# Layer two's experts: the product between the two halves comes out turned, with the first weights copied into fixed buffers and the expert's number loaded once per tile on VectorE

## The chip, the cores and the metric

The kernel runs on one core of a Trainium2 chip. The metric is the device time of one execution in microseconds (us). Engines are named as in the profile: PE (TensorE matmul), PEld (its weight loads), DVE (VectorE), ACT (ScalarE), POOL (GpSimd), SP (SyncE).

## What is computed

Four layers, each an attention and a feed-forward part, run over 32 sequences of 128 tokens with 128 features, all in float32. The change touches the feed-forward part of layer two, a mixture of eight experts of which each token uses the likeliest:

```
logits = jnp.einsum('bsd,de->bse', x, router_W) + router_b
probs = jax.nn.softmax(logits, axis=-1)
gates = one_hot(argmax(probs), 8) * probs
h = jax.nn.relu(jnp.einsum('bsd,edf->besf', x, W1) + b1[:, None, :])   # W1: 8 x 128 x 512
y = jnp.einsum('besf,efd->besd', h, W2) + b2[:, None, :]               # W2: 8 x 512 x 128
out = jnp.einsum('bse,besd->bsd', gates, y)
```

## The kernel before

Layer two (`layer2`) first does its attention for eight groups of four sequences, routes each token, and scatters the normalised token rows, sorted by expert, into `sorted_x` in DRAM. Each expert's rows fill whole tiles of 128 rows, so there are NTILE = 32 + 8 - 1 = 39 tiles. DVE works out, for each tile, its expert's number (`te`, an int32 row in SBUF) and its first row (`row`).

Then the tile loop runs on all five engines at once, each with its own hand-written order and semaphores between them. For tile u:

- SP loads the tile's 128 rows (`xt`, four buffers) once `turn_x` of tile u-4 is done (L1481 to L1485).
- PE `turn_x` (L1639) transposes them; ACT `xT_out` (L1776) copies the result to SBUF (`xT`, three buffers).
- DVE `add_b1` (L2013) loads the expert's number (L2006), adds the bias row of the expert, held in SBUF as a copy on each of the 128 partitions, and writes `hp` (two buffers).
- PE `turn_h` (L1654) transposes `hp` in four blocks of 128 (one pass each) into `bankH`, and ACT (L1784) applies the relu on the way to `hT` in SBUF (two buffers).
- PE `down` (L1663) loads the expert's number and multiplies with `l2f_w2`: four products of 128 columns summed in PSUM, eight passes, with the weights' address worked out in a register before each product.
- DVE `add_b2` (L2021) loads the expert's number and adds the second bias; POOL (L1823) stores the tile (`yt`, two buffers) to `routed_y`.

PE's order in step u of its loop is up(u+2), turn_x(u+3), turn_h(u+1), down(u). DVE's is add_b1(u+2), add_b2(u), and behind add_b2(2) it does eight small operations for the routing (`gates_and_places`, L2025 to L2033). ACT's is the relu of u, then xT_out(u+3). Layer three starts behind a barrier of all engines at the end of layer two.

Of the kernel before, what the change touches and what calls it, by code (L numbers as in the profile page):

```python
# [70 lines left out]
def seq(c):  # L71
    return slice(c * P, (c + 1) * P)
# [1251 lines left out]
def layer2(nc, k):  # L1324

    with ExitStack() as ctx:
# [63 lines left out]
        NX, NXT = 4, 3  # L1390
        xt = sb("x_tile", [P, NX, P], F32)
        xT = sb("xT_tile", [P, NXT, P], F32)
        hp = sb("h_tile", [P, 2, HID], F32)
        hT = sb("hT_tile", [P, 2, HID], F32)
        yt = sb("y_tile", [P, 2, P], F32)
# [1 line left out]
        bankX, bankS, bankAT, bankA, bankO, bankX2, bankM, bankR = (k.bank(i) for i in range(8))  # L1397
        bankL, bankK = bankR[:, 0:GS * NE2], bankR[:, 256:256 + GS * NE2]
        bankXT, bankU = [k.bank(0), k.bank(7)], [k.bank(1), k.bank(2)]
        bankH, bankY = [k.bank(3), k.bank(4)], [k.bank(5), k.bank(6)]  # L1400

        s_fill = sem("fills_done")
        s_row = sem("bias_row_ready")
# [46 lines left out]
        s_xt = [sem(f"x_tile_in_{p}") for p in range(NX)]  # L1450
        s_turn = sem("x_tile_turned")
        s_xT = sem("xT_tile_ready")
        s_up = sem("h_in_psum")
        s_hp = sem("h_tile_ready")
        s_turnh = sem("h_tile_turned")
        s_hT = sem("hT_tile_ready")
        s_y = sem("y_in_psum")
        s_yt = sem("y_tile_ready")
# [29 lines left out]
        def _(pe):  # L1488
# [150 lines left out]
                pe.transpose(bankXT[u % 2][:, 0:P], xt[:, u % NX, :], k.ident[:, :]).then_inc(s_turn, 1)  # L1639

            def up(u):
                e = expert(u)
                pe.wait_ge(s_xT, u + 1)
                if u >= 2:
                    pe.wait_ge(s_hp, u - 1)
                pe.matmul(bankU[u % 2][:, :], xT[:, u % NXT, :], w["l2f_w1"][:, bass.ds(e * HID, HID)], start=True,  # L1646
                          stop=True).then_inc(s_up, 1)

            def turn_h(u):
                pe.wait_ge(s_hp, u + 1)  # L1650
                if u >= 2:
                    pe.wait_ge(s_hT, u - 1)
                for n in range(NHB):
                    ins = pe.transpose(bankH[u % 2][:, seq(n)], hp[:, u % 2, seq(n)], k.ident[:, :])  # L1654
                ins.then_inc(s_turnh, 1)

            def down(u):
                e = expert(u)
# [9 lines left out]
                turn_x(u)  # L1668
            up(0)
            up(1)  # L1670
            turn_h(0)
            for u in range(NTILE):
                if u + 2 < NTILE:
                    up(u + 2)
                if u + 3 < NTILE:
                    turn_x(u + 3)
                if u + 1 < NTILE:
                    turn_h(u + 1)
                down(u)

        @block.scalar
        def _(act):
            k.wait_weights(act, "l2x")

            def normalise(dst, g, shift, rstd):
                for c in range(GS):
                    ins = act.activation(dst[:, c, :], k.x_sb[:, seq(g * GS + c)], ACT.Identity,
                                         bias=shift[:, g % 2, c:c + 1], scale=rstd[:, g % 2, c:c + 1])
                return ins

            def xn_in(g):
                act.wait_ge(s_shift1, g + 1)
                if g >= 3:
                    act.wait_ge(s_hbp, g - 2)
                normalise(xn[:, g % 3, :, :], g, shift1, rstd1).then_inc(s_xn, 1)

            def xnT_out(g):
                act.wait_ge(s_xp, g + 1)
                if g >= 3:
                    act.wait_ge(s_o, g - 2)  # L1700
                act.activation(xnT[:, g % 3, :], bankX[:, :], ACT.Copy).then_inc(s_xnT, 1)
                if g >= 2:
                    act.wait_ge(s_s, g - 1)
                act.activation(hwT[:, g % 2, :], bankX[:, :], ACT.Identity, bias=w["l2x_w2"][:, :],
                               scale=w["l2x_w3"][:, :]).then_inc(s_hw, 1)

            def exps(g):
                act.wait_ge(s_nmax, g + 1)
                if g >= 1:
                    act.wait_ge(s_attn, g)  # L1710
                for c in range(GS):
                    ins = act.activation(probs[:, c, :], bankS[:, seq(c)], ACT.Exp, bias=nmax[:, g % 2, c:c + 1],
                                         accum_out=total[:, c:c + 1])
                ins.then_inc(s_p, 1)

            def token_exp(g):
                act.wait_ge(s_m4, g + 1)
                if g >= 1:
                    act.wait_ge(s_pwp, g)
                act.activation(e4[:, :], bankM[0:GS, 128:256], ACT.Exp, bias=m4[:, :], accum_out=z4[:, :])\  # L1720
                   .then_inc(s_e4, 1)

            def attnT_out(g):
                act.wait_ge(s_atp, g + 1)
                if g >= 1:
                    act.wait_ge(s_a, g)
                act.activation(attnT[:, :], bankAT[:, :], ACT.Copy).then_inc(s_at, 1)

            def aT_out(g):
                act.wait_ge(s_a, g + 1)  # L1730
                if g >= 1:
                    act.wait_ge(s_o, g)
                act.activation(aT[:, :], bankA[:, :], ACT.Copy).then_inc(s_aT, 1)

            def h2_in(g):
                act.wait_ge(s_shift2, g + 1)
                normalise(h_all[:, rows(g)].rearrange("p (c d) -> p c d", c=GS), g, shift2, rstd2).then_inc(s_h2, 1)

            def hT2_out(g):
                act.wait_ge(s_h2p, g + 1)  # L1740
                if g >= 1:
                    act.wait_ge(s_lg, g)
                act.activation(hT2[:, :], bankX2[:, :], ACT.Copy).then_inc(s_hT2, 1)

            def gate_exp(g):
                act.wait_ge(s_sh, g + 1)
                act.activation(ex[:, g % 2, :], sh[:, g % 2, :], ACT.Exp).then_inc(s_ex, 1)

            xn_in(0)
            xn_in(1)  # L1750
            xnT_out(0)
            for s in range(last_step):
                if s < NG:
                    exps(s)
                if 2 <= s < NG + 2:
                    hT2_out(s - 2)
                if s < NG:
                    token_exp(s)
                if s + 1 < NG:
                    xnT_out(s + 1)  # L1760
                if s < NG:
                    attnT_out(s)
                if s + 2 < NG:
                    xn_in(s + 2)
                if 2 <= s < NG + 2:
                    gate_exp(s - 2)
                if s < NG:
                    aT_out(s)
                if 1 <= s < NG + 1:
                    h2_in(s - 1)  # L1770

            def xT_out(u):
                act.wait_ge(s_turn, u + 1)
                if u >= NXT:
                    act.wait_ge(s_up, u - NXT + 1)
                act.activation(xT[:, u % NXT, :], bankXT[u % 2][:, 0:P], ACT.Copy).then_inc(s_xT, 1)  # L1776

            for u in range(3):
                xT_out(u)
            for u in range(NTILE):  # L1780
                act.wait_ge(s_turnh, u + 1)
                if u >= 2:
                    act.wait_ge(s_y, u - 1)
                act.activation(hT[:, u % 2, :], bankH[u % 2][:, :], ACT.Relu).then_inc(s_hT, 1)  # L1784
                if u + 3 < NTILE:
                    xT_out(u + 3)

# [40 lines left out]
        def _(dve):  # L1828
# [176 lines left out]
            def expert(u):  # L2005
                return dve.value_load(te[0:1, u:u + 1], min_val=0, max_val=NE2 - 1)  # L2006

            def add_b1(u):
                e = expert(u)
                dve.wait_ge(s_up, u + 1)  # L2010
                if u >= 2:
                    dve.wait_ge(s_turnh, u - 1)
                dve.tensor_tensor(hp[:, u % 2, :], bankU[u % 2][:, :], w["l2f_b1"][:, bass.ds(e * HID, HID)], ALU.add)\  # L2013
                   .then_inc(s_hp, 1)

            def add_b2(u):
                e = expert(u)
                dve.wait_ge(s_y, u + 1)
                if u >= 2:
                    dve.wait_ge(s_out[u % 2], 16 * (u // 2))  # L2020
# [3 lines left out]
            def gates_and_places():  # L2024
# [7 lines left out]
                step(dve.scalar_tensor_tensor(pos_f[:, :], skip_all[:, :], -float(P), pos_f[:, :], ALU.mult, ALU.add))  # L2032
                dve.tensor_copy(k.routed_pos[:, :], pos_f[:, :])  # L2033

            add_b1(0)
            add_b1(1)
            for u in range(NTILE):
                if u + 2 < NTILE:
                    add_b1(u + 2)
                add_b2(u)  # L2040
                if u == 2:
                    gates_and_places()
# [847 lines left out]
class Global(Core):  # L2890
# [78 lines left out]
    def wait_weights(self, eng, layer):  # L2969
# [8 lines left out]
    "l1x": {"l1x_" + n: s for n, s in ATTN.items()},  # L2978
    "l0f": {"l0f_w1": [P, HID], "l0f_w2": [P, NHB, P], "l0f_cw": [P, 3 * HID], "l0f_cb": [P, NHB]},
    "l2f": {"l2f_router": [P, NE2], "l2f_router_b": [P, GS * NE2], "l2f_w1": [P, NE2 * HID],  # L2980
            "l2f_b1": [P, NE2 * HID], "l2f_w2": [P, NE2 * HID], "l2f_b2": [P, NE2 * P]},
    "l2x": {"l2x_w1": [P, 1], "l2x_w2": [P, 1], "l2x_w3": [P, 1], "l2x_bsim": [P, 1], "l2x_wqv": [P, 4, P],
            "l2x_bqv": [P, P]},
    "l3r": {"l3f_sim": [P, NE3], "l3f_gates": [P, NE3]},
# [109 lines left out]
def layouts(i):  # L3094
# [26 lines left out]
    d["l2f_router"] = f(i["L2_ffn_router_W"])  # L3121
    d["l2f_router_b"] = f(np.tile(i["L2_ffn_router_b"].reshape(1, NE2), (1, GS)))
    d["l2f_w1"] = f(np.transpose(i["L2_ffn_W1"], (1, 0, 2)).reshape(P, NE2 * HID))
    d["l2f_b1"] = f(i["L2_ffn_b1"].reshape(1, NE2 * HID))
    d["l2f_w2"] = f(np.transpose(i["L2_ffn_W2"].reshape(NE2, NHB, P, P), (2, 0, 1, 3)).reshape(P, NE2 * HID))
    d["l2f_b2"] = f(i["L2_ffn_b2"].reshape(1, NE2 * P))

# [41 lines left out]
```

## Time and profile before

| | us |
|---|---|
| median of three runs (1568.3, 1568.77, 1574.62) | 1568.77 |
| the profiled execution, its whole time | 1566.59 |
| its span in the profile | 1564.6 |
| lies around the span | 1.99 |
| PE busy in the span | 1371.5 (88%) |
| DVE / ACT / POOL busy | 852.7 / 546.8 / 417.6 |
| mean granted clock of PE | 0.916 |
| the tile loop, first `up` (862.9) to last `down` (962.3) | 99.4 |

The profile has for each engine the busy time, and for each group of instructions the line, the mean duration and the idle time before it with what ended it. Records of matmuls overlap, since PE is a pipeline: of a row that merges n equal passes, the distance between two starts is (the row's length minus the length of one record) / (n - 1).
### The profile page before, as it was taken

Reading aid. Unit: us, or ns where it says so; the run is one execution under the profiler, and the core shown is the slowest. Engines: PE = TensorE matmul, PEld = TensorE weight load, DVE = VectorE, ACT = ScalarE, POOL = GpSimd, SP = SyncE. Lnnn points to the kernel's source line nnn. Section 1 sums busy time; section 2 is a strip of 40 time slices with the busy share of each in tenths; the row PEclk is TensorE's granted clock in tenths of the full one; section 3 lists DMA queues with packets and bytes.
Section 4 is the critical chain, followed back from the end, with each engine's and each line's share of the span. In section 5 each row is a group of like instructions: output and inputs, shape, how many; then the busy total and the mean of one; then the engine's idle time right before and its main releaser. Section 6 shows DMA issues by size and latency. Waiting matters only on the chain. (4 is left out here: it accounts for less than half of the span.)

```text
span 1564.6 us, 26213 instructions
## 1 busy us (share of the span) xinstructions
PE 1371.5 (88%) x8915; PEld 847.1 (54%) x8915; DVE 852.7 (55%) x2511; ACT 546.8 (35%) x1291; POOL 417.6 (27%) x729
## 2 busy tenths in 40 slices
PE   5799886995899958996994996889999999999998
PEld 2477763552678845564883674554434444344443
DVE  5577645874577733333674433675554644546435
ACT  2366665662477732222661332350101101101011
POOL 3777601102677410001265122730000000000000
PEclk7799997996699979997896998699999999999999
DMA  6757640002777539100011112230220320202300
GB/s 183 177 143 163 154 109 0 1 1 69 168 171 178 133 147 418 55 1 21 21 38 34 49 55 73 103 123 1 108 115 1 115 89 27 115 29 86 115 0 14
DMA packets 73570, 140.94 MB, mean 90 GB/s; under 512 B 13302, under 2 KB 53750, under 8 KB 63590
## 3 DMA queue, kind: packets, MB, share of 16 engines
q1 hardware_dynamic: 66886, 131.79, 28.0%
q0 software_dynamic: 3296, 6.76, 1.3%
q8 instruction: 71, 1.16, 0.3%
q10 hardware_dynamic: 3264, 0.79, 0.3%
q14 instruction: 53, 0.43, 0.1%
HBM read 97.23 MB, written 41.09 MB: 88 GB/s over the span
## 5 line engine op out<-in xcount | busy, mean ns | idle before, releaser
L2761 DVE TENSOR_TENSOR l3f_weighted_T<-l3f_w_e,l3f_xnT 128x512 f32<-128x512 f32 x128 | 88.3, 691 | 116.6 <-PE psum L2340 109.6
L2340 PE MATMUL psum<-l3f_weighted_T,w_l3f_q 128*128 128x512 f32 x256 | 132.9, 601 | 10.3 <-DVE l3f_weighted_T L2761 8.6
L2340 PE MATMUL psum<-l3f_weighted_T,w_l3f_v 128*128 128x512 f32 x256 | 130.7, 592 | 0.0
L2340 PE MATMUL psum<-l3f_weighted_T,w_l3f_k 128*128 128x512 f32 x256 | 130.7, 592 | 0.0
L2349 PE MATMUL psum<-l3f_weighted_T,w_l3f_o 128*128 128x512 f32 x256 | 124.4, 624 | 2.1 <-DVE l3f_weighted_T L2761 2.1
L2761 DVE TENSOR_TENSOR l3f_weighted_T<-l3f_w_e,l3f_oT 128x512 f32<-128x512 f32 x128 | 88.3, 692 | 57.7 <-PE psum L2349 30.6
L707 DVE TENSOR_REDUCE l1x_minus_max<-psum 128x4 f32<-128x512 f32 x128 | 84.5, 686 | 55.8 <-PE psum L360 55.1
L707 DVE TENSOR_REDUCE l0x_minus_max<-psum 128x4 f32<-128x512 f32 x128 | 84.1, 685 | 36.8 <-PE psum L360 36.1
L111 POOL TENSOR_TENSOR l3f_ln_rstd<-l3f_ln_mean_var,eps 128x4 f32<-128x4 f32 x8 | 1.9, 242 | 331.2 <-DVE l3f_ln_mean_var L104 331.2
L2349 PEld LDWEIGHTS psum<-l3f_weighted_T,w_l3f_o 128*128 128x128 f32 x256 | 39.3, 188 | 83.2 <-DVE l3f_weighted_T L2761 78.6
L2340 PEld LDWEIGHTS psum<-l3f_weighted_T,w_l3f_v 128*128 128x128 f32 x256 | 48.6, 190 | 61.2 <-issue 61.2
L2340 PEld LDWEIGHTS psum<-l3f_weighted_T,w_l3f_k 128*128 128x128 f32 x256 | 48.6, 190 | 61.2 <-issue 61.2
L518 ACT ACTIVATE l0x_probsT<-psum 128x512 f32<-128x512 f32 x128 | 71.0, 601 | 22.8 <-PE psum L373 22.5
L518 ACT ACTIVATE l1x_probsT<-psum 128x512 f32<-128x512 f32 x128 | 70.8, 603 | 9.7 <-PE psum L373 9.3
L2340 PEld LDWEIGHTS psum<-l3f_weighted_T,w_l3f_q 128*128 128x128 f32 x256 | 44.0, 190 | 52.7 <-issue 42.5
L360 PE MATMUL psum<-l0x_k_stack,l0x_q_stack 72*128 72x128 bf16 x512 | 53.1, 231 | 7.6 <-DVE l0x_minus_max L707 3.7
L360 PE MATMUL psum<-l1x_k_stack,l1x_q_stack 72*128 72x128 bf16 x512 | 54.1, 234 | 1.9 <-DVE l1x_minus_max L707 1.5
L373 PE MATMUL psum<-l1x_q_stack,l1x_k_stack 75*128 75x128 bf16 x512 | 51.3, 224 | 4.5 <-DMA l1x_q_stack<-l1x_minus_max_T 2.9
L373 PE MATMUL psum<-l0x_q_stack,l0x_k_stack 75*128 75x128 bf16 x512 | 50.7, 223 | 2.9 <-DMA l0x_q_stack<-l0x_minus_max_T 2.8
L2013 DVE TENSOR_TENSOR l_h_tile<-psum,w_l2f_b 128x512 f32<-128x512 f32 x39 | 27.0, 692 | 40.4 <-PE psum L1646 39.3
L373 PEld LDWEIGHTS psum<-l1x_q_stack,l1x_k_stack 75*128 75x128 bf16 x512 | 35.3, 100 | 21.2 <-issue 13.2
L1646 PE MATMUL psum<-w_l2f_w,l_xT_tile 128*128 x78 | 44.9, 662 | 0.9 <-ACT l_xT_tile L1776 0.5
(488 smaller groups left out, 2951.5 us busy)
## 6 DMA issues: line engine op xcount, KB each, us to landing
l3f_w_e<-l3f_weights_scratch SPq DMA_DIRECT2D x32, 1024.0 KB, 4.6
sorted_x<-zeros SPq DMA_DIRECT2D x1, 16896.0 KB, 59.3
l0x_k_stack<-l0x_k_scratch SPq DMA_DIRECT2D x48, 192.0 KB
l0x_q_stack<-l0x_q_scratch SPq DMA_DIRECT2D x48, 192.0 KB
l1x_k_stack<-l1x_k_scratch SPq DMA_DIRECT2D x48, 192.0 KB
l1x_q_stack<-l1x_q_scratch SPq DMA_DIRECT2D x48, 192.0 KB
w_l2f_w<-in_l2f_w SPq DMA_DIRECT2D x2, 2048.0 KB, 13.4
l0x_k_scratch<-l0x_k_parts SPq DMA_DIRECT2D x16, 192.0 KB, 6.0
```

The source lines that it names most:

```text
L111: pool.tensor_tensor(k.rstd[:, :], k.mv[:, :, 1], k.eps[:, :], ALU.add).then_inc(k.s_vare, 1)
L360: ins = pe.matmul(bankS[u % 2][:, seq(i)], stack["q"][0:SROWS, g % 2, c // 2, h, of_seq(c)], stack["k"][0:SROWS, g % 2, c // 2, h, of_seq( ...
L373: ins = pe.matmul(bankT[u % 2][:, seq(i)], stack["k"][:, g % 2, c // 2, h, of_seq(c)], stack["q"][:, g % 2, c // 2, h, of_seq(c)], start=T ...
L518: act.activation(pT[:, j % 2, 4 * u:4 * u + 4, :], bankT[u % 2].rearrange("p (i q) -> p i q", i=4), ACT.Exp, scale=scale).then_inc(s_exp, 1)
L707: dve.tensor_reduce(nm[:, j % GS, 4 * u:4 * u + 4], bankS[u % 2].rearrange("p (i t) -> p i t", i=4), AX, ALU.max, negate=True).then_inc(s_ ...
L1646: pe.matmul(bankU[u % 2][:, :], xT[:, u % NXT, :], w["l2f_w1"][:, bass.ds(e * HID, HID)], start=True, stop=True).then_inc(s_up, 1)
L2013: dve.tensor_tensor(hp[:, u % 2, :], bankU[u % 2][:, :], w["l2f_b1"][:, bass.ds(e * HID, HID)], ALU.add)\
L2340: ins = pe.matmul(bank[:, :], w[name][:, e, :], xe[:, e % 2, :], start=(e == 0), stop=(e == NE3 - 1))
L2349: pe.matmul(bankO[g % 2][:, :], w["l3f_o"][:, e, :], xe[:, e % 2, :], start=(e == 0), stop=(e == NE3 - 1))\
L2761: dve.tensor_tensor(xe[:, e % 2, :], wE[:, g % 2, e, :], src, ALU.mult).then_inc(s_xe, 1)
```

## The change

- `up` swaps its operands: the stationary one is now the first weights in four blocks of 128 columns, the moving one is `xT` with 128 columns. Four products of 128 columns, eight passes, take the place of one of 512 columns, two passes. The hidden values come out turned: hidden units on the partitions, rows along the free axis.
- So `turn_h`, its semaphore and its two PSUM banks go. ACT's relu reads `hp` in SBUF.
- PE's stationary operand is read at a fixed address: DVE copies the expert's 128 x 512 block of `l2f_w1` into `w1t` (three buffers) with `take_w1`, for tiles 0 to 2 ahead of its loop and for u+3 at the start of step u, once `up` of tile u is done. PE's `up` has one wait more, for this copy, and no register work.
- DVE loads the expert's number once per tile, in `take_w1`, and keeps it in a register for add_b1 and add_b2.
- The first bias is laid out as one column per hidden block, 128 x 32 in place of 128 x 4096, and add_b1 reads it with a stride of zero along the rows. Its load shrinks from 2 MB to 16 KB.

```diff
             def up(u):
-                e = expert(u)
+                pe.wait_ge(s_w1t, u + 1)
                 pe.wait_ge(s_xT, u + 1)
                 if u >= 2:
                     pe.wait_ge(s_hp, u - 1)
-                pe.matmul(bankU[u % 2][:, :], xT[:, u % NXT, :], w["l2f_w1"][:, bass.ds(e * HID, HID)], start=True,
-                          stop=True).then_inc(s_up, 1)
-
-            def turn_h(u):
-                pe.wait_ge(s_hp, u + 1)
-                if u >= 2:
-                    pe.wait_ge(s_hT, u - 1)
                 for n in range(NHB):
-                    ins = pe.transpose(bankH[u % 2][:, seq(n)], hp[:, u % 2, seq(n)], k.ident[:, :])
-                ins.then_inc(s_turnh, 1)
+                    ins = pe.matmul(bankU[u % 2][:, seq(n)], w1t[:, u % 3, seq(n)], xT[:, u % NXT, :],
+                                    start=True, stop=True)
+                ins.then_inc(s_up, 1)
...
-                act.wait_ge(s_turnh, u + 1)
+                act.wait_ge(s_hp, u + 1)
                 if u >= 2:
                     act.wait_ge(s_y, u - 1)
-                act.activation(hT[:, u % 2, :], bankH[u % 2][:, :], ACT.Relu).then_inc(s_hT, 1)
+                act.activation(hT[:, u % 2, :], hp[:, u % 2, :], ACT.Relu).then_inc(s_hT, 1)
...
+            def take_w1(u):
+                e = expert_of[u] = expert(u)
+                if u >= 3:
+                    dve.wait_ge(s_up, u - 2)
+                dve.tensor_copy(w1t[:, u % 3, :], w["l2f_w1"][:, bass.ds(e * HID, HID)]).then_inc(s_w1t, 1)
+
             def add_b1(u):
-                e = expert(u)
+                e = expert_of[u]
                 dve.wait_ge(s_up, u + 1)
                 if u >= 2:
-                    dve.wait_ge(s_turnh, u - 1)
-                dve.tensor_tensor(hp[:, u % 2, :], bankU[u % 2][:, :], w["l2f_b1"][:, bass.ds(e * HID, HID)], ALU.add)\
+                    dve.wait_ge(s_hT, u - 1)
+                dve.tensor_tensor(hp[:, u % 2, :].rearrange("p (n t) -> p n t", n=NHB),
+                                  bankU[u % 2].rearrange("p (n t) -> p n t", n=NHB),
+                                  bcast(w["l2f_b1"][:, bass.ds(e * NHB, NHB)].unsqueeze(2), [P, NHB, P]), ALU.add)\
                    .then_inc(s_hp, 1)
...
+            for u in range(3):
+                take_w1(u)
             add_b1(0)
             add_b1(1)
             for u in range(NTILE):
+                if u + 3 < NTILE:
+                    take_w1(u + 3)
                 if u + 2 < NTILE:
                     add_b1(u + 2)
                 add_b2(u)
```

```order
L1633 TENSOR_LOAD l2_tile_expert
L1633 ISA x2
L1646 ISA
L1646 MATMUL psum<-w_l2f_w1,l2_xT_tile 128x512
L1639 MATMUL psum<-constants,l2_x_tile 128x128
L1654 MATMUL psum<-constants,l2_h_tile 128x128 x4
L1633 TENSOR_LOAD l2_tile_expert
L1633 ISA x2
L1663 ISA
L1663 MATMUL psum<-w_l2f_w2,l2_hT_tile 128x128
```

The same place after the change:

```order
L1648 MATMUL psum<-l2_xT_tile,l2_w1_tile 128x128 x4
L1640 MATMUL psum<-constants,l2_x_tile 128x128
L1634 TENSOR_LOAD l2_tile_expert
L1634 ISA x2
L1658 ISA
L1658 MATMUL psum<-w_l2f_w2,l2_hT_tile 128x128
```

Between two `down` there is one chain of register work in place of two, and four products in place of one product and four transposes. In `down` itself nothing moves.

DVE in one step of the loop before:

```order
L2006 TENSOR_LOAD l2_tile_expert
L2006 ISA x2
L2013 ISA
L2013 TENSOR_TENSOR l2_h_tile<-psum,w_l2f_b1 128x512
L2006 TENSOR_LOAD l2_tile_expert
L2006 ISA x2
L2021 ISA
L2021 TENSOR_TENSOR l2_y_tile<-psum,w_l2f_b2 128x128
```

The same place after the change:

```order
L1998 TENSOR_LOAD l2_tile_expert
L1998 ISA x2
L2006 ISA
L2006 COPY l2_w1_tile<-w_l2f_w1 128x512
L2013 ISA
L2013 TENSOR_TENSOR l2_h_tile<-psum,w_l2f_b1 128x512
L2023 ISA
L2023 TENSOR_TENSOR l2_y_tile<-psum,w_l2f_b2 128x128
```

The second load of the number is gone, and a copy of 128 x 512 stands ahead of the first addition.

## Rows read from the trace of the kernel before

**Rows 1.** Windows: busy time of each engine by stretch, passes in brackets, PE's clock

```profile
core 0: us, PE busy (x) PEld busy (x) DVE busy (x) ACT busy (x) POOL busy (x), PEclk, DMA share, GB/s
863.00:868.00 5.00, 5.00 (x13) 2.33 (x14) 1.38 (x2) 0.60 (x1) 0.00 (x0) 0.70 0.15 44
888.00:898.00 10.00, 10.00 (x61) 7.61 (x62) 4.03 (x9) 3.50 (x8) 2.15 (x4) 1.00 0.17 53
```

**Rows 2.** Timeline of one step: start, length, engine, line, passes, idle before and releaser

```profile
902.79 1.12 PE L1646 MATMUL psum<-w_l2f_w,l_xT_tile 128*128 x2
902.92 0.29 DVE L2021 TENSOR_TENSOR l_y_tile<-psum,w_l2f_b 128x128 f32<-128x128 f32 x1 [0.73 <-PE psum L1663]
903.51 0.54 POOL L1823 DMA_DIRECT2D routed_y<-l_y_tile  x1 [2.08 <-DVE l_y_tile L2021]
903.74 0.27 PE L1639 MATMUL psum<-constants,l_x_tile 128*128 128x128 f32 x1
903.85 0.60 PE L1654 MATMUL psum<-constants,l_h_tile 128*128 128x128 f32 x4
904.05 0.69 DVE L2013 TENSOR_TENSOR l_h_tile<-psum,w_l2f_b 128x512 f32<-128x512 f32 x1 [0.84 <-PE psum L1646]
904.29 1.06 PE L1663 MATMUL psum<-w_l2f_w,l_hT_tile 128*128 x8
904.49 0.60 ACT L1784 ACTIVATE l_hT_tile<-psum 128x512 f32<-128x512 f32 x1 [0.16 <-PE psum L1654]
```

**Rows 3.** Timeline, PE: the starts of up for tiles 2, 6, 7 and 38

```profile
866.75 0.69 PE L1646 MATMUL psum<-w_l2f_w,l_xT_tile 128*128 x1
...
876.51 1.12 PE L1646 MATMUL psum<-w_l2f_w,l_xT_tile 128*128 x2
...
880.26 0.69 PE L1646 MATMUL psum<-w_l2f_w,l_xT_tile 128*128 x1
...
957.04 1.12 PE L1646 MATMUL psum<-w_l2f_w,l_xT_tile 128*128 x2
```

**Rows 4.** Lines L1633, L2006: what loads the expert's number; ns min/median/max

```profile
L1633 PEldq TENSOR_LOAD <-l_tile_expert x78: 296/301/496, 861.9 to 960.3; - x78
L1633 PEldq FUSED_REGOPS  x78: 151/151/165, 862.5 to 960.7; - x78
L2006 DVEq TENSOR_LOAD <-l_tile_expert x78: 297/302/558, 853.0 to 961.2; - x78
```

**Rows 5.** Timeline at tile 3: DVE's routing steps from add_b2 on, and what waited

```profile
874.40 0.29 DVE L2021 TENSOR_TENSOR l_y_tile<-psum,w_l2f_b 128x128 f32<-128x128 f32 x1 [0.75 <-PE psum L1663]
...
876.55 0.18 DVE L2033 CAST routed_pos<-l_sorted_pos_f 128x32 int32<-128x32 f32 x1
...
877.37 0.69 DVE L2013 TENSOR_TENSOR l_h_tile<-psum,w_l2f_b 128x512 f32<-128x512 f32 x1 [0.64 <-issue]
```

**Rows 6.** Timeline, PE: the loop's start, and its end with two down running on

```profile
862.92 3.47 PE L1646 MATMUL psum<-w_l2f_w,l_xT_tile 128*128 x4 [0.53 <-ACT l_xT_tile L1776]
...
959.90 2.44 PE L1663 MATMUL psum<-w_l2f_w,l_hT_tile 128*128 x16
```

**Rows 7.** By line, 880.2 to 957.0, PEld: the weight loads of down

```profile
L1663 PEld LDWEIGHTS psum<-w_l2f_w,l_hT_tile 128*128 128x128 f32 x248 | 30.1, 192 | 0.0
```

**Rows 8.** Single lines of DVE from elsewhere: 128x512 from one source, and with a broadcast operand

```profile
L1011 DVE TENSOR_SCALAR l0f_w_steps<-l0f_w_steps x1: 427/427/427, 247.4 to 247.4; 128x512 f32<-128x512 f32 x1
L1876 DVE TENSOR_TENSOR l_attn<-l_probs,l_rtot x8: 691/728/779, 741.1 to 821.7; 128x512 f32<-128x512 f32 x8
```

**Rows 9.** Timeline before the loop: POOL issues scatters while DVE works on small tiles

```profile
850.70 0.96 POOL L1808 DMA_INDIRECT sorted_x<-l_h_all,l_sorted_pos  x1 [0.30 <-issue]
...
851.24 0.40 DVE L1997 TENSOR_SCALAR l_tile_expert_f<-l_tile_expert_f 128x39 f32<-128x39 f32 x1
851.67 0.18 DVE L1998 CAST l_tile_expert<-l_tile_expert_f 128x39 int32<-128x39 f32 x1
```

**Rows 10.** Barrier at the layer's end: POOL's drain

```profile
L1326 POOLq DRAIN  x2: 34/2948/5863, 965.1 to 971.7; - x2
```

More of the change, by code:

```diff
@@ L1392, in layer2 @@
         xT = sb("xT_tile", [P, NXT, P], F32)
+        w1t = sb("w1_tile", [P, 3, HID], F32)
         hp = sb("h_tile", [P, 2, HID], F32)
@@ L1399, in layer2 @@
         bankXT, bankU = [k.bank(0), k.bank(7)], [k.bank(1), k.bank(2)]
-        bankH, bankY = [k.bank(3), k.bank(4)], [k.bank(5), k.bank(6)]
+        bankY = [k.bank(5), k.bank(6)]
         s_fill = sem("fills_done")
@@ L1452, in layer2 @@
         s_xT = sem("xT_tile_ready")
+        s_w1t = sem("w1_tile_ready")
         s_up = sem("h_in_psum")
         s_hp = sem("h_tile_ready")
-        s_turnh = sem("h_tile_turned")
         s_hT = sem("hT_tile_ready")
@@ L1670, in _ @@
             up(1)
-            turn_h(0)
             for u in range(NTILE):
@@ L1676, in _ @@
                     turn_x(u + 3)
-                if u + 1 < NTILE:
-                    turn_h(u + 1)
                 down(u)
@@ L2006, in expert @@
                 return dve.value_load(te[0:1, u:u + 1], min_val=0, max_val=NE2 - 1)
+            expert_of = {}
+            def take_w1(u):
[3 more added lines that the diff above has]
+                dve.tensor_copy(w1t[:, u % 3, :], w["l2f_w1"][:, bass.ds(e * HID, HID)]).then_inc(s_w1t, 1)
             def add_b1(u):
-                e = expert(u)
+                e = expert_of[u]
                 dve.wait_ge(s_up, u + 1)
                 if u >= 2:
-                    dve.wait_ge(s_turnh, u - 1)
-                dve.tensor_tensor(hp[:, u % 2, :], bankU[u % 2][:, :], w["l2f_b1"][:, bass.ds(e * HID, HID)], ALU.add)\
+                    dve.wait_ge(s_hT, u - 1)
+                dve.tensor_tensor(hp[:, u % 2, :].rearrange("p (n t) -> p n t", n=NHB),
+                                  bankU[u % 2].rearrange("p (n t) -> p n t", n=NHB),
+                                  bcast(w["l2f_b1"][:, bass.ds(e * NHB, NHB)].unsqueeze(2), [P, NHB, P]), ALU.add)\
                    .then_inc(s_hp, 1)
             def add_b2(u):
-                e = expert(u)
+                e = expert_of[u]
                 dve.wait_ge(s_y, u + 1)
@@ L2980 @@
     "l2f": {"l2f_router": [P, NE2], "l2f_router_b": [P, GS * NE2], "l2f_w1": [P, NE2 * HID],
-            "l2f_b1": [P, NE2 * HID], "l2f_w2": [P, NE2 * HID], "l2f_b2": [P, NE2 * P]},
+            "l2f_b1": [P, NE2 * NHB], "l2f_w2": [P, NE2 * HID], "l2f_b2": [P, NE2 * P]},
     "l2x": {"l2x_w1": [P, 1], "l2x_w2": [P, 1], "l2x_w3": [P, 1], "l2x_bsim": [P, 1], "l2x_wqv": [P, 4, P],
@@ L3123, in layouts @@
     d["l2f_w1"] = f(np.transpose(i["L2_ffn_W1"], (1, 0, 2)).reshape(P, NE2 * HID))
-    d["l2f_b1"] = f(i["L2_ffn_b1"].reshape(1, NE2 * HID))
+    d["l2f_b1"] = f(i["L2_ffn_b1"].reshape(NE2 * NHB, P).T)
     d["l2f_w2"] = f(np.transpose(i["L2_ffn_W2"].reshape(NE2, NHB, P, P), (2, 0, 1, 3)).reshape(P, NE2 * HID))
```

## The prediction

> **What bounds the kernel now.** I read the windows first, to see who is full during the tile loop. From 888 to 898 PE is busy all 10.00 us at a granted clock of 1.00, while DVE is busy 4.03, ACT 3.50 and POOL 2.15 [rows 1]. So the loop goes at PE's pace, and the other engines' work is hidden. The timeline then says what PE's pace is made of [rows 2]. up starts at 902.79 and turn_x at 903.74, so up takes 0.95. turn_x to turn_h is 0.11. turn_h to down is 0.44 (903.85 to 904.29), four passes at (0.60 - 0.27) / 3 = 0.11. down's eight passes are (1.06 - 0.275) / 7 = 0.112 apart, 0.896 together. The four parts sum to 2.396 us per tile.
>
> The starts of up give the real pace [rows 3]: 876.51 - 866.75 = 9.76 for four steps, and 957.04 - 880.26 = 76.78 for 31 steps. That is 86.54 for 35 steps, or 2.473 each. The 0.077 above the sum is PE idling for an instruction that isn't there yet: in front of each up and each down its queue loads the expert's number, 0.301 plus 0.151 and gaps [rows 4], twice per tile. One step is out of line, tile 6 to tile 7, 880.26 - 876.51 = 3.75: DVE does the routing steps there from 874.40 to 876.73, then needs 0.82 from the start of its last one (876.55) to the next add_b1 (877.37), idle for "issue" 0.64 [rows 5], and PE waits. The number load causes that 0.82, a price I use below.
>
> Behind the loop comes a barrier in which POOL drains for 5.9 us [rows 10]. The number of its stores and scatters doesn't change, so I take the drain as constant, and what the loop gains the whole kernel gains.
>
> **The change part by part, PE.** turn_h goes: -0.44 per tile. up becomes eight passes of 128 columns, each with its own weight load. down is exactly that form, eight float32 passes with 128 x 128 weights and 128 moving columns, at 0.112, though one of its weight loads lasts 0.192 [rows 2, 7]; loads and passes overlap. So up costs 8 x 0.112 = 0.896 in place of 0.95. turn_x and down stay. The new sum is 0.896 + 0.11 + 0.896 = 1.90.
>
> To this comes what the queue of PE adds. up has no register work left, since w1t lies at a fixed address. down keeps one number load, about 0.8 with its gaps by the price above. It can be hidden behind the 1.00 us of up and turn_x in front of it. That leaves little room, so now and then something shows. The lower bound is 0; the upper is the gap between two down that run on without work in between: 16 passes last 2.44 where 15 x 0.112 + 0.275 = 1.96 would do, so at most 0.48 [rows 6]. I take 0.05, near the 0.077 that two such loads cost per step today. That makes 1.95.
>
> The Trainium skill ("TensorE: Matmul & The Clock Gate", Back-to-back issue gap) speaks against narrow passes: it gives about 81 ns for a pass of 128 columns and about 131 ns for one of 512. An estimate from that page makes up 8 x 0.081 - 2 x 0.131 = 0.39 dearer per tile, which eats nearly all that turn_h gives. The rows of this kernel show 0.112 for 128 columns and about 0.48 for 512 (0.95 / 2), a ratio of four, and I go by them.
>
> **DVE.** The second number load goes. The copy of 128 x 512 comes, a form the trace doesn't have. The nearest row is a one-source operation on 128 x 512, 0.427 [rows 8]. From below I bound it by half of that, from above by the two-source 0.69 of add_b1 [rows 2]. I take 0.43. add_b1 with its bias of stride zero stays at 0.69; L1876 with a broadcast operand has a median of 0.728 [rows 8], 0.04 more and hidden. add_b2 is 0.29. If nothing overlaps, DVE's step is 0.82 from the start of add_b2 over the number to the start of the copy, then 0.43 and 0.69, with two hand-overs of 0.06: 2.06. That is over PE's 1.95. It would bind only if DVE couldn't load the number while add_b1 still runs; busy time alone is 0.43 + 0.69 + 0.29 = 1.41.
>
> Then the latency. In step u the copy for tile u+4 comes behind add_b2(u), which starts 0.3 behind the end of down(u) (902.92 against 902.79 for the up that follows [rows 2]; the gap in front of that up is the rest). So the copy starts 0.3 + 0.82 = 1.12 and ends 1.55 behind the end of down(u). PE needs it at the end of down(u+1), 1.90 behind. It is in time by about 0.3. This is the thinnest margin of the change. Queued behind the copy on DVE stands add_b1(u+3), which PE needs only two steps later, by up(u+5). Queued behind PE's wait for the copy stand up, turn_x and down.
>
> **ACT** reads hp in SBUF where it read PSUM, 0.60 [rows 2], and starts 0.44 earlier in the chain. Its step is 0.28 + 0.60, hidden. Of the DMAs, SP's x tile is asked for four tiles ahead, and POOL's store has two tiles' time, 3.9 us, for 0.54 of issue and its landing: both hidden. The load of the first bias shrinks by 2 MB, but it is issued at 571, some 290 us ahead of its use, and no engine waits for it: nothing. The three copies ahead of the loop lie in DVE's idle time before 862.92, when PE waits for the first rows: nothing.
>
> **Start, routing step, end.** At the start up(2) waits for add_b1(0) and turn_h(0), until 866.75 [rows 3]; without turn_h it can follow up(1) directly: -0.4. PE's clock is 0.70 there [rows 1] as it warms, before and after alike. At the routing step the copy for tile 6 now stands behind the routing steps: 0.3 + (876.55 - 874.40) + 0.82 + 0.43 + 0.06 = 3.8 behind the end of down(2), where PE wants it at 1.9. So that step is 3.85 in place of 3.75: +0.1. At the end, from up(38) to the last pass, 959.90 + 2.44 - 957.04 = 5.30 becomes 4 x 0.896 + 0.17 + 0.5 of uncovered number loads = 4.25: -1.05.
>
> **The sum.** 35 x (2.473 - 1.95) = 18.3. With 0.4 + 1.05 - 0.1 that is 19.65. The profiled execution is 1566.59 (span 1564.6 and 1.99 around it) and would become 1546.9. The median of the runs shown is 1568.77, 2.2 above it; it would become **1549.1**. With 1.90 per step it is 1547.4, with DVE's 2.06 it is 1553.
>
> **Rivals.**
> 1. DVE's chain becomes the bound. In the scatter part a one-source operation on 39 columns took 0.40 and ended within 0.02 of POOL's issue (850.70 + 0.96), where the cast of the same size behind it took 0.18 [rows 9]: it was held up by POOL's issue. The Trainium skill ("Advanced Engine Details and Errata", VectorE Performance Modes) has it that DVE's two-port modes and GpSimd block each other; the trace agrees, 0.22 longer. In the loop POOL's issue runs from 0.59 to 1.13 behind the start of add_b2 [rows 2], and the copy would start at 0.82: up to 0.31 lost. The chain of 2.06 becomes 2.37 at most. At 2.2 per step: 35 x 0.27 + 1.35 = 10.8 saved, 1558. Against it speak the 0.3 of margin and that DVE is idle 60% of the time.
> 2. Narrow passes cost more than in down, say because there a number load in between hides them. At the 0.192 of a weight load up would be 1.54 and the step 2.54, slower; at half that surcharge 2.23. The page's 0.39 gives a step of 2.473 - 0.44 + 0.39 = 2.42 by an estimate. I put this case at about 1566. The down row speaks against it.
> 3. Slower: DVE's chain closes with PE's in a ring. If the copy runs at 0.69 with 0.31 of POOL, and DVE waits 0.3 for down's end and 0.3 for up's end one after the other, the step is 2.06 + 0.26 + 0.31 + 0.3 = 2.93 at worst. It decides from 2.51 per step (2.473 + 1.35 / 35). At 2.8: 35 x 0.33 - 1.35 = 10 lost, 1579. The three buffers speak against it: no wait of PE is on the step before.
> 4. The change does what it says but PE's clock falls to 1.2 GHz where PE waits for copies. The clock was 0.50 only around stretches with idle PE; at the start two up took 3.47 us [rows 6] in place of 1.9, so the loop would lose some 40 us. Rare.
>
> **How the numbers follow.** Forecast, 1547 to 1554: 0.75. Rival 1, 1554 to 1562: 0.13. Rival 2, around 1566: 0.07. Rivals 3 and 4: 0.05. The range goes from 1545.5, a little below the 1547.4 of the bare sum for the spread of the runs (1568.3 to 1574.6), to 1558, which takes in the likelier half of rival 1. About 0.5% (7.8 us) is what a measurement of this kernel can tell from no change: faster is the forecast and most of rival 1, 0.87; within it the rest of rival 1 and rival 2, 0.08; slower 0.05.
>
> **What would show it.** In the trace of the changed kernel: 39 x 8 passes of up at 0.112 distance; starts of up(u) and up(u+1) 1.90 to 2.0 apart with granted clock 1.00; turn_h gone; PE waiting for the copy only at tile 6, for some 1.9 us; the copy at about 0.43; the last down around 942.5; the 5.9 us drain unchanged; layer three starting some 20 us earlier and lasting as long. It is wrong if PE's idle time names the copy in every step (rival 1 or 3), if the passes of up stand more than 0.12 apart (rival 2), or if the copy lasts over 0.7.

## The result and the profile after

The changed kernel took 1552.53 us (median of four, 1548.64 to 1555.37) where the kernel before took 1571.01 on the same chip (1568.3 to 1574.62). The ratio is 0.988, with an interval of 0.9845 to 0.9915. The forecast was 1549.1 from 1568.77, a ratio of 0.9875. The profiled execution took 1548.64 (span 1546.6) against 1546.9 forecast.

The windows of the kernel after, the view of [rows 1] (columns as there), show that PE is still busy all 10.00 us at clock 1.00. It now does 92 passes in 10 us where it did 61. DVE's work went from 4.03 to 6.88:

```profile
888.00:898.00 10.00, 10.00 (x92) 10.00 (x91) 6.88 (x16) 3.98 (x10) 3.63 (x5) 1.00 0.24 71
```

The timeline of one step of the kernel after answers to [rows 2]. L1648 is up, L1640 turn_x, L1658 down, L2006 the copy, L2013 add_b1, L2023 add_b2:

```profile
900.14 1.06 PE L1658 MATMUL psum<-w_l2f_w,l_hT_tile 128*128 x8
...
901.04 1.06 PE L1648 MATMUL psum<-l_xT_tile,l_w_tile 128*128 128x128 f32 x8
...
901.35 0.29 DVE L2023 TENSOR_TENSOR l_y_tile<-psum,w_l2f_b 128x128 f32<-128x128 f32 x1
...
901.93 0.27 PE L1640 MATMUL psum<-constants,l_x_tile 128*128 128x128 f32 x1
...
901.93 0.73 POOL L1815 DMA_DIRECT2D routed_y<-l_y_tile  x1 [1.12 <-DVE l_y_tile L2023]
902.04 1.06 PE L1658 MATMUL psum<-w_l2f_w,l_hT_tile 128*128 x8
902.11 0.43 DVE L2006 COPY l_w_tile<-w_l2f_w 128x512 f32 x1 [0.47 <-PE psum L1648]
...
902.41 0.62 ACT L1776 ACTIVATE l_hT_tile<-l_h_tile 128x512 f32<-128x512 f32 x1
902.46 0.69 DVE L2013 TENSOR_TENSOR l_h_tile<-psum,w_l2f_b 128x512 f32<-128x512 f32 x1
902.83 0.97 PEld L1648 LDWEIGHTS psum<-l_xT_tile,l_w_tile 128*128 128x128 f32 x8
902.93 1.06 PE L1648 MATMUL psum<-l_xT_tile,l_w_tile 128*128 128x128 f32 x8
```

From up to up is 902.93 - 901.04 = 1.89: up 0.89, turn_x 0.11, down 0.89, nothing between them. The copy ends at 902.54. PEld starts to load up's weights, which the copy wrote, at 902.83, and the first pass follows at 902.93. So the margin is 0.29 to the weight load and 0.39 to the pass.

PE's timeline gives the length of the loop, from the first pass of up(0) to the last of down(38). Its first and last lines, and the starts of up(6), up(7) and up(38):

```profile
865.12 4.62 PE L1648 MATMUL psum<-l_xT_tile,l_w_tile 128*128 128x128 f32 x24
...
878.06 1.16 PE L1648 MATMUL psum<-l_xT_tile,l_w_tile 128*128 128x128 f32 x8 [1.63 <-DVE l_w_tile L2006]
...
880.05 1.06 PE L1648 MATMUL psum<-l_xT_tile,l_w_tile 128*128 128x128 f32 x8
...
940.00 1.06 PE L1648 MATMUL psum<-l_xT_tile,l_w_tile 128*128 128x128 f32 x8
...
940.90 3.40 PE L1658 MATMUL psum<-w_l2f_w,l_hT_tile 128*128 x24
```

The loop lasts 944.30 - 865.12 = 79.2, where before it lasted 959.90 + 2.44 - 862.92 = 99.4 [rows 6]. That is 20.2 less; 19.65 was forecast. Of this, 18.0 is in the span. The loop started 2.2 later: layer one's attention, which the change doesn't touch, took 3.9 longer in this execution (last section), and the other stages ahead of the loop 1.7 less. The barrier came 0.6 later behind the loop, and layer three took 0.5 less. POOL's drain is as it was [rows 10]:

```profile
L1326 POOLq DRAIN  x2: 34/2948/5863, 947.6 to 954.3; - x2
```

### The profile page after: what moved, and what is told of

Its sections match the earlier page's. It is cut to its first block and busy times, and to the rows that moved or that the text cites. A ratio compares the mean times of both kernels' runs of the same rounds, so it can differ in the third digit from the quotient of the medians.

```text
span 1546.6 us, 26139 instructions
## 1 busy us (share of the span) xinstructions
PE 1350.3 (87%) x8993; PEld 851.9 (55%) x8993; DVE 866.3 (56%) x2550; ACT 544.6 (35%) x1291; POOL 422.5 (27%) x729
## 5 line engine op out<-in xcount | busy, mean ns | idle before, releaser
L373 PEld LDWEIGHTS psum<-l1x_q_stack,l1x_k_stack 75*128 75x128 bf16 x512 | 35.8, 101 | 20.2 <-issue 8.9
L360 PEld LDWEIGHTS psum<-l0x_k_stack,l0x_q_stack 72*128 72x128 bf16 x512 | 36.7, 104 | 15.1 <-issue 8.8
L1648 PE MATMUL psum<-l_xT_tile,l_w_tile 128*128 128x128 f32 x312 | 43.1, 284 | 2.1 <-DVE l_w_tile L2006 2.1
```

What stands on the lines that cost most here:

```text
L360: ins = pe.matmul(bankS[u % 2][:, seq(i)], stack["q"][0:SROWS, g % 2, c // 2, h, of_seq(c)], stack["k"][0:SROWS, g % 2, c // 2, h, of_seq( ...
L373: ins = pe.matmul(bankT[u % 2][:, seq(i)], stack["k"][:, g % 2, c // 2, h, of_seq(c)], stack["q"][:, g % 2, c // 2, h, of_seq(c)], start=T ...
L1648: ins = pe.matmul(bankU[u % 2][:, seq(n)], w1t[:, u % 3, seq(n)], xT[:, u % NXT, :], start=True, stop=True)
```

## The experiments

The whole time of one kernel spreads by up to 20 us (the 21 runs of before from 1563.36 to 1580.4, the ten of "copy only" from 1552.92 to 1573.25), while the two traces of the kernel after have loops of 79.2 and 80.0. So each trace is read by its loop. "Step" is the median distance between the first passes of up. The routing step is the longest one near tile 6, when DVE does its routing steps. The tail runs from the start of up(38) to the last pass.

| kernel | time, us (n) | ratio to before, interval | loop | step | routing step | tail |
|---|---|---|---|---|---|---|
| before | 1571.01 (4) | 1 | 99.4 | 2.457 (mean 2.473) | 3.75 | 5.3 |
| after | 1552.53 (4) | 0.988, 0.9845 to 0.9915 | 79.2 | 1.896 | 3.69 | 4.30 |
| number loaded in up | 1555.56 (6) | 0.9911, 0.9868 to 0.9953 | 88.8 | 2.20 | 3.49 | 4.59 |
| copy only | 1566.33 (10) | 0.9962, 0.9924 to 0.9999 | 93.7 | 2.30 | 3.69 | 5.21 |
| number loaded thrice | 1567.31 (10) | 0.9982, 0.9957 to 1.0007 | 99.5 | 2.467 | 4.56 | 4.82 |
| copy doubled | 1552.93 (4) | 0.9873, 0.9819 to 0.9928 | 85.7 | 2.07 | 4.17 | 4.72 |
| after, again | 1547.55 (6) | 0.9859, 0.9823 to 0.9894 | 80.0 | 1.896 | 3.69 | 4.30 |
| copy on ACT | 1543.85 (1) | one run | 77.1 | 1.896 | 2.57 | 4.36 |
| four y buffers | 1555.94 (1) | one run | 79.4 | 1.896 | 4.04 | 4.30 |
| ACT and four y | 1545.41 (6) | 0.9847, 0.9813 to 0.9881 | 77.0 | 1.896 | 2.58 | 4.35 |

The first two rows are the result above. Beside the four experiments from "number loaded in up" to "copy doubled" the kernel before took 1568.57 (21 runs), and 1568.16 (11 runs) beside the last four; the ratios are to these. The ratios are coarser than the loops: the intervals of "number loaded in up" and "copy doubled" overlap that of the kernel after, though their loops are 9.6 and 6.5 longer. But each loop is that of a single execution.

### Is PE's number load cheap?

The forecast put two number loads per step at 0.077. If so, putting the second one back would hardly show. In PE's up, with its value unused:

```
             def up(u):
...
+                expert(u)
```

> The changed kernel, but PE loads the expert's number once more in front of each up and doesn't use it. In the changed kernel a step (start of up to start of the next up) is 1.896 us and the tile loop (first up to last down) 79.2. My theory as predicted: passes set PE's pace and number loads hide behind them, at most 0.04 each, so the step stays between 1.90 and 1.94, the loop at 79 to 81, the time within 2 us of the changed kernel's (1552.5). Rival: it is PE's own queue of waits, number loads and address work that set the pace of the kernel before (2.473 against 2.396 of passes), and one load is 0.30 + 0.15 + gaps, some 0.65; then the second load puts the step at 2.2 to 2.4, the loop at 91 to 98, and the time at 1563 to 1570.

Measured: 2.20 per step in place of 1.896, so 0.30 for one load; the loop is 88.8. PE's timeline of this kernel (L1649 is up, L1659 down), and a line of its weight loads:

```profile
901.81 1.08 PE L1659 MATMUL psum<-w_l2f_w,l_hT_tile 128*128 x8
902.90 1.13 PE L1649 MATMUL psum<-l_xT_tile,l_w_tile 128*128 128x128 f32 x8
903.87 0.27 PE L1640 MATMUL psum<-constants,l_x_tile 128*128 128x128 f32 x1
903.98 1.08 PE L1659 MATMUL psum<-w_l2f_w,l_hT_tile 128*128 x8
```

```profile
902.87 0.97 PEld L1649 LDWEIGHTS psum<-l_xT_tile,l_w_tile 128*128 128x128 f32 x8 [0.17 <-issue]
```

From down to up is 1.09 where it was 0.89, and from up to turn_x 0.97 where it was 0.89. PE's weight load waits for "issue" ahead of up. So my price was wrong. The rival that I wrote down for this run is nearer, that PE's queue with its waits, number loads and addresses sets the pace once it holds two loads in so short a step. Its step of 2.2 to 2.4 was met at the lower end, but its loop of 91 to 98 and its time of 1563 to 1570 were not (88.8 and 1555.56). One load hides in the step of 1.896, two don't. The second one stood right in front of up; another place for it wasn't tried.

### Which half of the change brings what?

The kernel before, with the copy and the single number load on DVE, and with turn_h and the two passes of 512 columns kept:

```
             def up(u):
-                e = expert(u)
+                pe.wait_ge(s_w1t, u + 1)
...
-                pe.matmul(bankU[u % 2][:, :], xT[:, u % NXT, :], w["l2f_w1"][:, bass.ds(e * HID, HID)], start=True,
+                pe.matmul(bankU[u % 2][:, :], xT[:, u % NXT, :], w1t[:, u % 3, :], start=True,
                           stop=True).then_inc(s_up, 1)
```

> The kernel before with the copy of the first weights and one number load per tile on DVE alone: up still streams 512 columns, now from the fixed buffer, and turn_h stays. If the swapped product and the missing turn_h carry the gain (my theory), the step falls only from 2.473 to the bare sum of passes, 2.40 to 2.42, with the routing step a little longer: 2 to 3 us off the time before. If taking register work off PE's queue is what carries it (rival), the step falls below 2.3 and over 6 us go. The start of up's second pass tells whether the 0.53 us of the first pass of up (0.43 for the second) belongs to the address in a register.

Measured: 2.30 per step, loop 93.7. PE's timeline of this kernel (L1648 up, L1641 turn_x, L1656 turn_h, L1665 down):

```profile
900.64 0.60 PE L1656 MATMUL psum<-constants,l_h_tile 128*128 128x128 f32 x4
...
901.08 1.06 PE L1665 MATMUL psum<-w_l2f_w,l_hT_tile 128*128 x8
...
901.97 1.02 PE L1648 MATMUL psum<-l_w_tile,l_xT_tile 128*128 128x512 f32 x2
...
902.83 0.27 PE L1641 MATMUL psum<-constants,l_x_tile 128*128 128x128 f32 x1
```

down is 0.89, up 0.86, turn_x 0.11, turn_h 0.44: they sum to 2.30, with no idling left. The step lies between the 2.40 to 2.42 of my theory and the "below 2.3" of the rival, and the loop is 5.7 shorter; my theory missed that part of the gain lies inside up. The run splits the 0.577 of a step (2.473 - 1.896). Taking the number load and the register-held address out of PE's up gives 0.17: 0.09 of it as up falls from 0.95 to 0.86, the rest the 0.077 of idling.

The 0.09 needs no register-held address. At the routing step of this same kernel, where up reads the fixed buffer but PE waited for the copy, up takes 0.96 again:

```profile
878.82 1.12 PE L1648 MATMUL psum<-l_w_tile,l_xT_tile 128*128 128x512 f32 x2 [1.23 <-DVE l_w_tile L2016]
879.78 0.27 PE L1641 MATMUL psum<-constants,l_x_tile 128*128 128x128 f32 x1
```

In the kernel after, too, up takes 0.99 to 1.00 in place of 0.89 at each of the four places where PE had to wait for the copy after the loop's start. When PE's queue is in time, up's first weight load runs under the pass in front of it (902.83 against 902.93 above). When the queue or the copy is late, load and pass start together, and the second pass comes 0.10 later. In the kernel before they started together in every up from up(2) on. So the 0.17 is the price of a queue that comes late, and a number load in front of up makes it late; what the address alone adds wasn't tried. Turning the product gives the other 0.40 of the 0.577: turn_h's 0.44 less 0.04, since eight narrow passes take 0.896 where two wide ones take 0.86. That 0.04 is what narrow passes cost. By the page's figures that the prediction weighed (the Trainium skill, "TensorE: Matmul & The Clock Gate", Back-to-back issue gap) it would have been an estimated 0.39; the measurement decides.

The swap without the copy would leave the stationary operand of up at an address held in a register, and was not tried.

### Is DVE near its limit, and by its work or by its latency?

DVE loads the number for the copy, for add_b1 and for add_b2, as three loads per tile:

```
             def add_b1(u):
-                e = expert_of[u]
+                e = expert(u)
...
             def add_b2(u):
-                e = expert_of[u]
+                e = expert(u)
```

> The changed kernel, but DVE loads the number again ahead of add_b1 and of add_b2, three times per tile. In the trace of before two additions with a number load between them start 0.83 us apart although the operation itself is shorter. Theory that DVE's chain of number loads can bind: three such distances are 2.49 us per step, over PE's 1.90, so the step is 2.3 to 2.5, the loop 92 to 99 us, the time 1565 to 1572. Rival, that the loads hide behind DVE's own operations (busy 1.41 us) and PE still sets the pace: step 1.90 to 2.0, time within 3 us of the changed kernel's.

Measured: 2.467 per step, the loop as long as before (99.5; the ratio of the times is 0.9982, 0.9957 to 1.0007), though DVE's arithmetic is the same. Its timeline:

```profile
900.44 0.43 DVE L2006 COPY l_w_tile<-w_l2f_w 128x512 f32 x1 [0.48 <-issue]
...
900.92 0.97 PEld L1648 LDWEIGHTS psum<-l_xT_tile,l_w_tile 128*128 128x128 f32 x8 [0.44 <-DVE l_w_tile L2006]
...
901.28 0.69 DVE L2013 TENSOR_TENSOR l_h_tile<-psum,w_l2f_b 128x512 f32<-128x512 f32 x1 [0.41 <-issue]
...
902.16 0.29 DVE L2023 TENSOR_TENSOR l_y_tile<-psum,w_l2f_b 128x128 f32<-128x128 f32 x1 [0.19 <-issue]
...
902.92 0.43 DVE L2006 COPY l_w_tile<-w_l2f_w 128x512 f32 x1 [0.47 <-issue]
```

Start to start it is 0.84, 0.88 and 0.76, in the mean 0.83, nearly the 0.82 that the prediction read from [rows 5]. It is about the same behind operations of 0.43, 0.69 and 0.29: the load starts as soon as the operation in front of it has started and runs beside it, but the next operation starts some 0.8 behind that one's start (0.75 at the least from 884 to 955). Three such hand-overs are the step. "Loaded once per tile" is therefore a condition of the gain.

The second run adds work and no load: every copy is made twice.

```
+                dve.tensor_copy(w1x[:, u % 3, :], w["l2f_w1"][:, bass.ds(e * HID, HID)])
                 dve.tensor_copy(w1t[:, u % 3, :], w["l2f_w1"][:, bass.ds(e * HID, HID)]).then_inc(s_w1t, 1)
```

> The changed kernel with a second copy of the first weights per tile, into a buffer that nobody reads, ahead of the real one: 0.43 us more on DVE per tile. Predicted margin theory: the copy is there 0.39 us before PE wants it, and what is over eats into a ring of two steps, so the step becomes 1.90 to 1.97, the loop 79.5 to 82, the time 0 to 3 us more. Rival: the chain of DVE doesn't overlap with itself (2.06 us by the sum of the prediction) and binds: 2.06 + 0.43 = 2.49 per step, loop 98, the time about 1573.

Measured: steps of 1.90 and 2.08 in turn, some of 2.2 to 2.5, a routing step of 4.17 with one of 3.62 behind it, and a loop of 85.7. My theory was right in kind: the late copy has two steps to recover, so 0.43 more work costs 0.09 in the mean of the regular pairs and not 0.6. It was too small in size: a step of 1.90 to 1.97 and a loop of 79.5 to 82 were expected. One reason is that I had measured the margin to the first pass, 0.39, and not to its weight load, 0.29: the copy, 0.34 later, comes too late for the load, and up then has its uncovered 0.10 as well. Where add_b2 came late for another reason, nothing was left to take it up:

```profile
900.92 0.29 DVE L2025 TENSOR_TENSOR l_y_tile<-psum,w_l2f_b 128x128 f32<-128x128 f32 x1 [0.40 <-DMA routed_y<-l_y_tile]
...
901.69 0.43 DVE L2007 COPY l_w_again<-w_l2f_w 128x512 f32 x1 [0.48 <-issue]
902.03 0.43 DVE L2008 COPY l_w_tile<-w_l2f_w 128x512 f32 x1
...
902.51 0.97 PEld L1649 LDWEIGHTS psum<-l_xT_tile,l_w_tile 128*128 128x128 f32 x8 [0.57 <-DVE l_w_tile L2008]
```

### Can the rest of the copy's cost be had?

In the kernel after, a few ordinary steps are longer. At 920 the chain runs from a store that hasn't landed, over add_b2 and the copy, to PE:

```profile
918.99 0.29 DVE L2023 TENSOR_TENSOR l_y_tile<-psum,w_l2f_b 128x128 f32<-128x128 f32 x1 [0.68 <-DMA routed_y<-l_y_tile]
...
920.12 0.43 DVE L2006 COPY l_w_tile<-w_l2f_w 128x512 f32 x1 [0.83 <-issue]
...
920.60 1.05 PE L1648 MATMUL psum<-l_xT_tile,l_w_tile 128*128 128x128 f32 x7 [0.43 <-DVE l_w_tile L2006]
```

Two experiments cut this chain, at its start (four buffers `yt` in place of two) and in its middle (the copy on ACT, with ACT's own number load, behind relu). The third does both.

```
-        yt = sb("y_tile", [P, 2, P], F32)
+        yt = sb("y_tile", [P, 4, P], F32)
```

```
+            def take_w1(u):
+                e = act.value_load(te[0:1, u:u + 1], min_val=0, max_val=NE2 - 1)
+                if u >= 3:
+                    act.wait_ge(s_up, u - 2)
+                act.activation(w1t[:, u % 3, :], w["l2f_w1"][:, bass.ds(e * HID, HID)], ACT.Copy).then_inc(s_w1t, 1)
```

> The changed kernel, but ACT makes the copy of the first weights (with a number load of its own), behind the relu of u, while DVE loads the number once per tile for its two additions. Theory: at the routing step (3.68 us in the changed kernel) PE waits only because the copy stands behind DVE's routing steps; with the copy on ACT that step falls to 1.9 to 2.1, the ordinary step stays 1.90, and the loop goes from 79.2 to 77 to 77.6. POOL's issue of a store, 0.73 us in the changed kernel against 0.54 before, returns to 0.54, since it was DVE's copy that it collided with. Rival: it is add_b1 behind the routing steps that PE waits for, then the routing step stays at 3.5 or more; or ACT's chain (0.28 + 0.62 + 0.60 and a number load) binds, then the step is over 2.0.

> The changed kernel with four buffers for the output tile instead of two. In the changed kernel add_b2 waited 8 times, 5.5 us in all, for the landing of an earlier store, and steps of 2.49 and 2.14 follow two of these waits; the last down waits for nothing of it, but the last two add_b2 do, about 1.2 us each. Theory: the steps of 2.49 and 2.14 are gone (0.9 us of the loop), and the last add_b2 comes within 0.4 us behind the last down instead of about 0.8: the loop falls from 79.2 to 78.0 to 78.5, the routing step stays near 3.7. Rival: those steps come from late number loads or x tiles and stay.

> Both together: the copy on ACT and four buffers for the output tile. Sum of the two theories: loop 76.2 to 77 against 79.2, the whole time 2 to 3 us below the changed kernel's, some 21 us below the kernel before. The spread of the whole times (about 10 us between runs) is larger than that difference, so the loop in the trace decides.

Measured: with four buffers the steps of 2.49 and 2.14 are gone, but in that execution one step at the loop's start took 2.98 and the routing step 4.04, so the loop is 79.4 where 78.0 to 78.5 was expected; why these two were longer isn't shown. With the copy on ACT the loop is 77.1, inside the 77 to 77.6 expected. The routing step gives 1.1 of it and comes to 2.57, between the 1.9 to 2.1 of my theory and the 3.5 of the rival: there PE waits for add_b1 and no longer for the copy.

```profile
878.12 0.69 DVE L2021 TENSOR_TENSOR l_h_tile<-psum,w_l2f_b 128x512 f32<-128x512 f32 x1 [0.99 <-PE psum L1648]
...
878.96 1.13 PE L1648 MATMUL psum<-l_xT_tile,l_w_tile 128*128 128x128 f32 x8 [0.51 <-DVE l_h_tile L2021]
```

Both together give 77.0, the same, so with ACT's copy the two further buffers add nothing that one trace of each can show. The whole time is 1545.41 against 1547.55 for the kernel after beside it. The traces show 3.0 less in the loop (77.0 against 80.0), but the intervals of the ratios overlap, so the times don't settle it.

## Why the prediction was right, step by step

**The sum.** From up(2) to up(38), without the routing step, 35 steps took 67.8 (1.94 in the mean, 1.896 as median) where they took 86.5: 18.8 gained, 18.3 forecast. The start gave 0.4 (up(0) to up(2) in 3.42 where it was 3.83), as forecast; the tail 1.0, forecast 1.05. The routing step went from 3.75 to 3.69, where +0.1 was forecast. The sum is 20.2.

**PE.** turn_h's 0.44 and the 0.112 of a narrow pass held. "0.05 for an uncovered number load" was wrong both ways. The one load left shows nothing at all (1.896 is the bare 1.90), and its reason, that a load costs PE some 0.04, fell in the first experiment: it costs 0.30 when a second one is there. The bound of 0.48 that I took for a far upper end was nearer to that. I had read the 0.95 of up as two passes; 0.09 of it was a weight load that came too late to be covered, as "copy only" shows. The total came out right all the same, since the old step was measured whole (2.473) and the ordinary new one had no idle time in it: how the difference divides between the load, the address and turn_h doesn't enter it. That the mean step was forecast at 1.95 and came to 1.936 is in part luck: the 0.05 stood for number loads that show nothing, and the 0.04 above the bare sum came from late stores and copies, which the prediction held to be hidden.

**DVE.** The copy took 0.427 as median, as the row of one-source work [rows 8] said; add_b1 stayed at 0.69. "If nothing overlaps, 2.06" did not bind: DVE's chain from add_b2 to add_b2 is as long as PE's step, because it waits for PE. add_b2 starts 0.31 behind PE's change from down to up (901.35 against 901.04; 0.3 was forecast), the copy 0.76 behind it (0.82), and the copy ends 1.50 behind the change (1.55). PE's first pass wants it at 1.89 and its weight load at 1.79, so the margin is 0.29 to the load; "about 0.3" was forecast, but to the pass, where it is 0.39. The sign that PE would wait for the copy "only at tile 6" failed: it also waited at tiles 10, 28 and 34, whose steps were 0.02, 0.59 and 0.24 longer.

**ACT** took 0.62 for the relu where 0.60 stood, and it is hidden. The larger miss was the store of the result: "two tiles' time, hidden" was 3.9 at 1.95 per step, and add_b2 waited for a store eight times, 5.5 in all from the first tile to the last. This reached PE only in the few longer steps; all that is longer than 1.896 sums to 1.4 of the loop (35 x (1.936 - 1.896)), 0.14 of it at the loop's start. Three of the eight waits, 3.1 of the 5.5, stand at the loop's end. There add_b2(38), after waiting 1.17 for a store, started 0.75 behind PE's last pass where it was 0.15 before, which is the barrier's 0.6. With four buffers it started 0.15 behind again, but POOL's drain came no earlier behind the last pass in that one execution (3.5, where it was 3.3 after and 2.7 before), so what the buffers are worth at the barrier stays open.

**Rival 1** (collision with POOL's issue): it happened, but to POOL. The grouped rows of POOL's store, first of before, then of after, then with the copy on ACT:

```profile
L1823 POOL DMA_DIRECT2D routed_y<-l_y_tile x22 | 11.8, 538 | 42.6 <-DVE l_y_tile L2021 42.6
```

```profile
L1815 POOL DMA_DIRECT2D routed_y<-l_y_tile x28 | 19.4, 692 | 34.9 <-DVE l_y_tile L2023 34.9
```

```profile
L1826 POOL DMA_DIRECT2D routed_y<-l_y_tile x30 | 16.1, 538 | 39.5 <-DVE l_y_tile L2031 39.5
```

The issue takes 692 ns in the mean where it took 538, and 538 again once the copy is off DVE, while the copy stays at 0.427. Of the 39 issues 28 took 0.72 to 0.74: in these the copy began 0.17 to 0.19 behind the start of the issue, and the issue ended 0.12 behind the copy's end (901.93 + 0.73 against 902.11 + 0.43 in the step shown above). Where the copy began before the issue, or 0.26 behind its start, the issue took 0.54 although the two overlapped. So it is the moment of the meeting that counts, and in the loop it is POOL that waits, though its issue began first; POOL has the time. That the two engines block each other, as the page has it (the Trainium skill, "Advanced Engine Details and Errata", VectorE Performance Modes), the trace agrees with, 0.18 longer. The other direction, which the prediction read from [rows 9], is borne out by a second trace: the operation that took 0.40 there, begun 0.54 behind the start of POOL's scatter issue, took 0.18 in the second trace of the kernel after, where it began 0.26 behind one.

**Rival 2** was worth 0.04 per step and not 0.64 or 0.32. **Rival 3** didn't occur; the doubled copy shows how far off it was, and the number loaded thrice shows what would have brought it about. **Rival 4:** PE's clock is 1.00 throughout the steady loop.

## What to carry to other kernels

Count register loads as work of the engine that does them: here a second one per step cost PE 0.30 us, and on DVE each put 0.8 between the starts of two operations, so load once per tile and keep the value for every use. Turning a product by exchanging its operands costs little where the pass time goes with the columns (0.896 against 0.86 here), and it drops the transposes. Here a copy on an engine with idle time gave the stationary operand a fixed address; whether it must have one wasn't tried. Measure the margin of such a copy to the weight load that reads it, not to the pass. When a loop gets a fifth faster, look at the buffers whose release depends on a DMA: two were enough at 2.47 per step and just short at 1.90.

## What the runs showed of the hardware

The variation between runs has its place in these traces. From 500 to 550, in layer one's attention, before any changed line runs, PE's granted clock was 1.00 in some executions and 0.93 in others (columns as in [rows 1]); here before, then after:

```profile
500.00:550.00 50.00, 47.69 (x803) 39.48 (x801) 35.78 (x77) 36.73 (x84) 21.62 (x57) 1.00 0.59 140
```

```profile
500.00:550.00 50.00, 44.93 (x717) 36.77 (x717) 31.75 (x68) 32.19 (x73) 18.88 (x49) 0.93 0.61 126
```

From PE's first pass of layer one's attention to its last, the four traces at 1.00 (before, number loaded in up, after again, ACT and four y) took 194.5 to 198.4 us, and the four at 0.93 (after, copy doubled, copy on ACT, four y) 201.5 to 209.8. The two others fit in less neatly: "number loaded thrice" had 0.97 and 198.4, "copy only" 0.86 and 203.3. The same kernel, after, took 202.3 in one execution and 194.5 in another. Why an execution gets the one or the other wasn't tried. In the two rows shown the lower clock and more idle time of PE go together, and which comes first stays open. It is why the loop's length, and not the whole time, carries the readings above.

The other surprise is the price of a number load on PE. It looked like 0.04 in the step of 2.47. Taking up's load and address away there gave 0.17, since a weight load that isn't covered adds 0.10 inside up, where it doesn't look like idle time. In the step of 1.90 a load put in front of up cost 0.30. What an instruction seems to hide at one pace is no measure of what it costs at another.
